# Attention's order by thirds: one scaling, Pool's share of the values, the turnings and the low rank stand in later thirds

## The reference

```
xn = layernorm(x)
s  = mamba_like_block(xn)                # first stage of the kernel, 1024 channels, state of 16
# FFN block on xn:
r   = rmsnorm(xn, ln1)                   # "rows"
q, k, v = r @ Wq.T, r @ Wk.T, r @ Wv.T   # 16 heads of 32
p   = softmax(causal(q @ k.T / sqrt(32)))
mod = 0.1 * tanh((p @ v) @ Wo.T @ A)     # A: 512 x 16, so low rank
h   = rmsnorm(xn, ln2)
gate = silu(h @ W_in.T + mod * (h @ A) @ B)
f   = xn + (gate * (h @ W_up.T)) @ W_down.T
out = x + s * silu(f)
```

## Time and profile before

| what | value |
|---|---|
| median of 3 runs | 2691.47 us (2690.93 to 2692.01) |
| the profiled execution, its own time | 2695.38 us |
| its span, first to last instruction | 2693.6 us |
| mean granted TensorE clock | 0.975 |
| PE busy | 2517.1 us, 93% |
| DVE busy | 1408.0 us, 52% |
| ACT busy | 1075.3 us, 40% |
| Pool busy | 353.0 us, 13% |

### The profile page before, as it was taken

One profiled execution on the slowest core, in us unless ns is written; L12 is line 12 of the kernel. 1 busy time (PEld: TensorE's weight loads), 2 busy tenths in 40 slices (PEclk: granted clock), 3 DMA queues, 4 the chain that ended last, 5 costly groups with the idle time before them and its releaser, 6 DMA issues.

```text
span 2693.6 us, 38693 instructions
## 1 busy us (share of the span) xinstructions
PE 2517.1 (93%) x14359; PEld 2024.4 (75%) x14359; DVE 1408.0 (52%) x2927; ACT 1075.3 (40%) x1776; POOL 353.0 (13%) x356
## 2 busy tenths in 40 slices
PE   4799999999999699999999879999999999999997
PEld 3677777777778576776777658888888788888886
DVE  6666566566555387787878853222222523333333
ACT  3444444444444267776777752111111311111111
POOL 0000000000000133334433320000000001111111
PEclk9899999999999799999999979999999999999999
DMA  4000000000003344434444411111111402222212
GB/s 135 16 17 17 32 16 17 32 6 27 16 1 114 107 132 126 130 82 121 132 122 118 142 48 71 47 47 47 48 47 71 164 32 94 94 94 94 94 63 78
DMA packets 97760, 194.63 MB, mean 72 GB/s; under 512 B 22144, under 2 KB 22656, under 8 KB 91408
## 3 DMA queue, kind: packets, MB, share of 16 engines
q1 hardware_dynamic: 96160, 190.24, 22.5%
q10 hardware_dynamic: 1408, 1.84, 0.3%
HBM read 99.43 MB, written 41.94 MB: 52 GB/s over the span
## 4 chain that ended last, share of the span: by engine, by line
PE 53%; DVE 3%; SPq 3%; POOL 2%; issue 2%; DMA 1%; ACT 1%; ACTq 1%; DVEq 0%; POOLq 0%
PE PS L72 9%; PE PS L74 9%; PE PS L73 9%; PE PS L1933 4%; PE PS L1935 4%; PE PS L1934 4%; SPq L1509 3%; PE PS L1577 2%; PE PS L1596 2%; PE PS L1554 2%; PE PS L1556 1%; PE PS L1555 1%; DMA STGB<-in_x_dram 1%; PE PS L1915 1%; POOL PL L1780 1%
## 5 line engine op out<-in xcount | busy, mean ns | idle before, releaser
L1982 DVE TENSOR_TENSOR GF<-SG,PS 128x512 f32<-128x512 f32 x128 | 88.0, 687 | 619.6 <-PE PS L74 619.6
L1722 DVE CUSTOM_DVE_ANT_0 PS<-PS,MK 128x512 f32<-128x512 f32 (+3 forms) x512 | 243.5, 505 | 119.8 <-PE PS L1577 118.7
L1956 ACT ACTIVATE SG<-PS 128x512 f32<-128x512 f32 x128 | 76.3, 596 | 429.1 <-PE PS L1915 429.0
L1674 ACT ACTIVATE PF<-PS 128x512 f32<-128x512 f32 (+1 forms) x384 | 199.4, 527 | 105.3 <-PE PS L1598 89.1
L1960 ACT CAST GH<-GF 128x512 fp32r<-128x512 f32 x128 | 79.4, 620 | 365.0 <-DVE GF L1982 365.0
L72 PE MATMUL PS<-XH,WH 128*128 128x512 f32 x512 | 211.3, 413 | 6.4 <-DVE XC L976 6.4
L72 PE MATMUL PS<-FH,GW 128*128 128x512 f32 x512 | 200.0, 391 | 7.7 <-DVE DW L1977 7.7
L1933 PE MATMUL PS<-DW,GH 128*128 128x512 f32 x512 | 200.3, 391 | 4.7 <-DVE GL L1984 4.7
L2013 POOL TENSOR_SCALAR XN<-XT,MEAN,RSTD 128x512 f32<-128x512 f32 x32 | 66.6, 2085 | 1041.6 <-DMA M<-m_scratch 727.3
L74 PE MATMUL PS<-XH,WL 128*128 128x512 f32 x512 | 202.6, 396 | 0.0
L73 PE MATMUL PS<-XL,WH 128*128 128x512 f32 x512 | 202.2, 395 | 0.0
(11 more groups left out here) (277 smaller groups left out, 5822.6 us busy)
## 6 DMA issues: line engine op xcount, KB each, us to landing
QS<-QT SPq DMA_DIRECT2D x384, 64.0 KB, 2.0
KS<-QT SPq DMA_DIRECT2D x360, 64.0 KB, 2.0
FH<-rh_scratch SPq DMA_DIRECT2D x16, 1024.0 KB, 5.9
FL<-rl_scratch SPq DMA_DIRECT2D x16, 1024.0 KB, 7.9
XF<-in_x_dram SPq DMA_DIRECT2D x32, 256.0 KB, 3.3
s_scratch<-ZS SPq DMA_DIRECT2D x8, 1024.0 KB, 4.4
rh_scratch<-RH SPq DMA_DIRECT2D x8, 1024.0 KB, 8.6
rl_scratch<-RL SPq DMA_DIRECT2D x8, 1024.0 KB, 10.6
```

Of the source, the lines that this page charges most:

```text
L1674: act.activation(PE_[u][:, o:o + at], PS[4 + a % 2][:, 0:at], ACT.Exp, scale=SC).then_inc(a_ex, 1)
L1722: dve.tensor_tensor_reduce(out=p[:, at:at + n], in0=p[:, at:at + n], in1=MK[:, 512 - n:512], scale=1.0, scalar=NEG, op0=ALU.add, op1=ALU.m ...
```

## The change

Four things move in attention's order:
- `scaled` number 0 goes from third -38 to third -34 of the batch (third 10 to third 14 counted from the batch before).
- The four `normal` steps go from thirds -2, -1, 1, 2 to thirds -3, 0, 1, 3; their banks stay 0, 1, 0, 1, and each `normal_low` stays one third behind its own.
- Pool's two operations on the values get a step of their own, `values_end`, two thirds behind `values_low`, where they stood; DVE's part stays in `values_low`.
- `low_rank` goes from third 44 to third 45. For the next batch these are thirds -4 and -3.

```diff
-            for k, third in enumerate((-38, -26, -17, -8)):
+            for k, third in enumerate((-34, -26, -17, -8)):
                 if b:
                     at(t + third, "scaled", b, k)
-            for d, third, bank in ((0, -2, 0), (1, -1, 1), (2, 1, 0), (3, 2, 1)):
+            for d, third, bank in ((0, -3, 0), (1, 0, 1), (2, 1, 0), (3, 3, 1)):
                 bank_of["normal", b, d] = bank
                 if b:
                     at(t + third, "normal", b, d)
...
                 at(t + third, "values", b, J)
                 at(t + third + 1, "values_low", b, J)
+                at(t + third + 3, "values_end", b, J)
             bank_of["low_rank", b] = 1
-            at(t + 44, "low_rank", b)
+            at(t + 45, "low_rank", b)
...
-                elif kind == "values_low":
+                elif kind == "values_end":
                     n, V = 4 * a + how, VB[a % 2]
                     v3 = V1[:, how % 2, :].rearrange("p (h r) -> p h r", r=R)
                     pool.wait_ge(a_v1, n + 1)
```

## The result

| what | before | after |
|---|---|---|
| median of the runs | 2691.74 us (4 runs) | 2661.48 us (4 runs, 2656.63 to 2663.3) |
| ratio, 95% interval | | 0.9882 (0.9865 to 0.99) |
| profiled execution, its own time | 2695.38 us | 2661.16 us |
| its span | 2693.6 us | 2659.3 us |
| PE busy | 2517.1 us | 2508.9 us |

The ratio is 31.8 us less, with 27 to 36 us inside its interval; the medians differ by 30.3 us, the two profiled executions by 34.2 us. In the changed kernel every line behind 1304 is one higher (from the change on).

A forecast was written before the change was run, and what follows sets the result against it. PE was taken as the one engine near its limit, so time comes out only where it waits or runs slowly; 19.2 + 9.2 + 2.8 = 31.2 us less gave a median of 2660 us, range 2652 to 2672.

The forecast's parts named there:

- Scaling 0: Attention, third 10 to 14: PE's waits for Pool's remainder and the clock falls after them go in five batches, 19.2 us.
- Pool's third term: Attention's values: with values_end behind the next remainder, PE's 21 other waits for Pool in seven batches go, 9.2 us.
- The lean stretch: Thirds 42 to 52, low rank and turnings moved: 0.46 us gained in each of six batches, 2.8 us.
- The clock: Attention's thirds 15 to 22: each fall of PE from 2.4 to 1.2 GHz after a long wait costs 1.7 us.
- DVE's waits vanish unreplaced: Rival, lean stretch: PE's waits for DVE go with nothing in their place, 10.8 instead of 2.8 us, 2652 us; 12%.
- The lean stretch gets worse: Rival, lean stretch: -6 instead of +2.8 us, as PE waits for maxima before the low rank, 2669 us; 10%.
- The wait for XB moves on: Rival, third 18: XB landing 3 us later costs five batches 1.5 us each, 7.5 us, 2668 us; 8%.
- Pool collides with DVE: Rival, moved Pool operations: they hold up DVE by 0.38 us each where it is full, 13 us, 2673 us; 4%.
- Slower than before: Rival, lean stretch: low rank and turning back to back starve ACT and DVE, clock falls, 2701 us; 3%.
- no change: Rival, Pool's moved steps: Pool is blocked for another reason and PE waits as before, 2691 us; 3%.

The follow-up runs named there:

- e4: Kernel before with scaling 0 alone moved to third 12, still ahead of Pool's remainder of third 13; ratio 0.9992, -2 us.
- e9: Whole change, but scaling 0 in third 13 and values_end one third behind values_low; ratio 0.9891 against the kernel before, -29 us.
- e2: Kernel before with only Pool's part of the values (values_end) two thirds later; ratio 0.9955, -12.1 us.
- e5: Kernel before with scaling 0 and values_end moved, low rank and turnings left in place; ratio 0.9902, -26 us.
- e3: Kernel before with only the low rank in third 45 and the turnings in -3, 0, 1, 3; ratio 1.0014, +3.8 us.
- e8: The whole change run again against the kernel before; ratio 0.9893, -29 us.
- e6: e5 with the low rank also moved to third 45; ratio 0.9904 against the kernel before, -26 us.
- e12: e9 with the low rank split into four parts in thirds 44 and 45; ratio 0.9892 against the kernel before, -29 us.

## Why the prediction was right

2660 us were forecast and 2661.5 measured, 31.2 us less against 31.8 by the ratio. The mechanism of each of Pool's two moves held. That the sum came out within 2 us is in part luck, since one term was too small and two too large: 19.2 + 9.2 + 2.8 were forecast, and the parts measured 18.6, 12.1 and 2.0. Point by point:

- *Scaling 0, 19.2 us.* Right: 18.6 us alone (15 to 22), and the stretches of thirds 15 to 22 lost 19.1 us beyond the 0.55 us of the values. All falls of the clock in attention's steady part went. That only the place against the remainder of third 13 counts is shown by e4 and e9. XB lands as before, as forecast; the slack in third 18 was more than the 1.5 us forecast (remainder ready at 1203.70, PE at about 1206.2), and no wait for Pool came back. Two signs were put wrong. Thirds 15 to 22 were to take 11.5 us and take 11.0, for third 21's share of the values' term lies in them. And Pool's wait for XB was to stay at 8 us and is 4.6 us, because Pool now does a remainder first.
- *Pool's third term, 9.2 us.* Right in mechanism, mis-sized: 12.1 us by time, 11.8 by the lengths of e2's batches 0 and 6. The term was the sum of the listed waits, and those are short by the overlap of the record before them, 0.14 us each.
- *The lean stretch, 2.8 us.* The sum was near: 0.5 us in each of five periods and 0.4 in the sixth, less 0.9 us in batch 0: 2.0 us (e5 against the kernel after). The prediction said that batch 0's steps run before the first weights and cost nothing; but batch 0's low rank and the turnings of the next batch's rows stand around those weights, and with the low rank in third -3 PE waits 0.9 us for maxima ahead of it there. The new wait stands where forecast (line 1578 for maxima, 0.71 us as listed against 1.1 forecast, low rank at 1172.8, which is 1186.6 on the clock of the batch before the change against 1186.7 forecast), and no falls of the clock with it. But the working didn't ask which of the two moves earns it: the turnings do, and all of it. And the sum took for granted that the terms add. Timed by itself the lean part costs 3.8 us (e3), for a reason that stays open.
- *The clock.* The forecast took 1.7 us for each fall. 2.4 and 1.2 GHz are the two levels in these rows, and in e3, where all five waits are between 2.65 and 2.81 us, the three stretches of thirds 15 to 22 with a fall take 15.9 to 16.1 us and the two without 14.3 and 14.4: 1.6 us.
- *Rivals.* "DVE's waits vanish unreplaced" falls: they were replaced by the wait for maxima, and e5 to e8 show 0.5 of 1.7 us gained a batch. "The lean stretch gets worse" falls: 21.4 us against 22.1, and in e3, which is slower, 21.55. "The wait for XB moves on" happened by 0.1 to 0.3 us in single batches of the kernel after, e6 and e9 to e12, through V and not through the remainder. "Pool collides with DVE" is real and small: that same V comes late because line 1730 takes 1.38 us beside Pool's row of steps instead of 1.22, and up to 1.5 us in the kernel after and 1.7 in e6 where XB lands late. "Slower than before" and "no change" fall.

The 33.0 us that batches 0 to 6 lost (555.3 to 522.3) went to the end whole, the spans differing by 34.3; the feed-forward stage starts with nearly the same wait for DVE's weights, 7.7 us before and 7.8 after.

## What to carry to other kernels

In a hand-written order, put an in-order helper's step that waits for something slow behind the next step that others wait for; how far behind is of little matter. Read such a wait's price from the length of the stretch with and without it, not from the listed wait: the listed one leaves out the overlap of the record before it and the clock it costs afterwards. And remove a wait whose end another engine sets before earning time ahead of it: here the same two moves measured 3.8 us slower with that wait in place, and about 2 us faster without it by the lengths in the traces. Why they cost time in the first case isn't shown.

## What was not expected of the hardware

**Waits of the same length.** In the kernel before, three of the five long waits of `mixed` were 2.65 us to within 3 ns, though XB landed 24.3 to 24.7 us after third -1. The same 2.65 us stands three times in e2, twice in e4 and once in e3. DVE's line 1729 in the batch of the earlier trace rows:

```profile
1216.41 1.22 DVE L1729 TENSOR_TENSOR PL<-PF,PH 128x1024 f16<-128x1024 f32 x1
```

Pool's remainder, started at 1217.09, ends at 1218.15, 0.52 us after this DVE instruction does: it seems to be held until DVE is through, so the landing within that span doesn't matter. In the next batch Pool started first, and DVE was held instead:

```profile
1297.53 0.67 POOL L1780 TENSOR_TENSOR PL<-PF,PH 128x256 f16<-128x256 f32 x1
```
```profile
1297.81 1.47 DVE L1729 TENSOR_TENSOR PL<-PF,PH 128x1024 f16<-128x1024 f32 x1
```

Pool 0.67 and DVE 1.47 us there, Pool 1.06 and DVE 1.22 us here. That is what the Trainium skill says in "SBUF — State Buffer", section "Who interferes with whom": a DVE instruction with two SBUF inputs and a GpSimd instruction that reads SBUF shut each other out, and the order of issue decides who waits. The trace agrees as to who waits. Shut out for the whole overlap, Pool would have lost 0.54 us and DVE 0.39; they lost 0.39 and 0.25.

**The clock after such a wait.** Of 14 waits of 2.65 us or more for the scaling in the traces of four kernels (before 4, e2 3, e3 5, e4 2) 10 were followed by a fall from 2.4 to 1.2 GHz; of five of 1.0 to 1.5 us none was. The length alone doesn't decide: the three waits of 2.65 us in the kernel before all had a fall behind them, and of three of 2.65 us in e2 one had. Whether such waits make a kernel vary more from run to run isn't shown.
